# Attention block: output products of each head group in one slot, both key halves together

## What is computed

```python
q, k, v = qkv of _gn(x)
attn = jnp.einsum('bqd,bkd->bqk', q * scale, k)
attn = attn + rel_h[:, :, :, :, None] + rel_w[:, :, :, None, :]   # from q and two tables
attn = jax.nn.softmax(attn, axis=-1)
out = jnp.einsum('bqk,bkd->bqd', attn, v)
x = x + (out @ proj_w + proj_b)
```

## Time and profile before

| | |
|---|---|
| median of 3 runs | 1974.27 us (1973.04 to 1978.66) |
| the profiled execution's own time | 1973.15 us |
| its span, first to last instruction | 1971.3 us |
| mean granted TensorE clock | 0.996 |
| TensorE busy | 1904.9 us (97%) |
| VectorE, ScalarE, GpSimd busy | 1436.1, 1364.7, 713.3 us |
| `ps_o` matmuls | 6144 records, 340 ns each on the mean |

### The profile page before, as it was taken

The page is one execution under the profiler, slowest core; times in us unless marked ns, Lnnn a source line. Parts: engine busy times, 40 slices in busy tenths (PEclk is TensorE's granted clock), DMA queues, the critical chain, the costliest instruction groups (busy, mean ns, idle before and its releaser), DMA issues.

```text
span 1971.3 us, 85928 instructions
## 1 busy us (share of the span) xinstructions
PE 1904.9 (97%) x34944; PEld 1558.5 (79%) x34944; DVE 1436.1 (73%) x3566; ACT 1364.7 (69%) x3201; POOL 713.3 (36%) x1796
## 2 busy tenths in 40 slices
PE   0799999999999999999999999999999999999998
PEld 0688888888888888888888888888888888888885
DVE  6477777777777777777777777777777777777774
ACT  0277777777777777777777777777777777777775
POOL 0333433334334334334334333343343343343331
PEclk9999999999999999999999999999999999999999
DMA  1434444444444444444344344444444444444430
GB/s 38 101 93 110 103 100 110 103 102 108 104 100 109 103 102 107 102 107 105 100 110 104 99 110 106 100 104 108 100 107 104 101 108 102 107 104 100 112 97 23
DMA packets 142177, 197.86 MB, mean 100 GB/s; under 512 B 26455, under 2 KB 109656, under 8 KB 141786
## 3 DMA queue, kind: packets, MB, share of 16 engines
q1 hardware_dynamic: 141786, 192.36, 39.3%
HBM read 97.74 MB, written 57.80 MB: 79 GB/s over the span
## 4 chain that ended last, share of the span: by engine, by line
PE 93%; issue 3%; DVE 2%; POOL 1%; ACT 0%; DMA 0%; POOLq 0%; SPq 0%; DVEq 0%; ACTq 0%
PE ps_m L402 24%; PE ps_max L511 17%; PE ps_o L543 17%; PE ps_sc L524 13%; PE ps_m L463 10%; PE ps_m L477 6%; PE ps_m L419 2%; PE ps_m L487 2%; PE ps_m L468 1%; PE ps_m L425 1%; DVE k_st L658 0%; POOL yo L837 0%; DVE v_st L651 0%; POOL xn L814 0%; POOL xn_lo L827 0%
## 5 line engine op out<-in xcount | busy, mean ns | idle before, releaser
L701 DVE TENSOR_REDUCE mx<-ps_max 98x2 f32<-98x392 f32 x1536 | 834.9, 558 | 237.3 <-PE ps_max L511 223.4
L574 ACT ACTIVATE probs<-ps_sc 98x392 f32<-98x392 f32 x1536 | 735.4, 496 | 216.8 <-PE ps_sc L524 171.8
L511 PE MATMUL ps_max<-k_st,q_st 124*98 124x196 f16 x3072 | 538.1, 257 | 0.6 <-DVE mx L701 0.3
L524 PE MATMUL ps_sc<-q_st,k_st 125*98 125x196 f16 x3072 | 511.7, 247 | 0.6 <-ACT probs L574 0.5
L511 PEld LDWEIGHTS ps_max<-k_st,q_st 124*98 124x98 f16 x3072 | 293.8, 125 | 200.1 <-issue 157.6
L543 PE MATMUL ps_o<-probs,v_st 98*32 98x196 f32 x6144 | 388.7, 340 | 2.0 <-issue 1.2
L524 PEld LDWEIGHTS ps_sc<-q_st,k_st 125*98 125x98 f16 x3072 | 320.9, 124 | 3.4 <-ACT probs L574 1.8
L752 DVE TENSOR_TENSOR rel_hl<-ps_m,rel_hi 128x504 f16<-128x504 f32 (+1 forms) x384 | 216.2, 563 | 85.5 <-ACT rel_hi L619 85.5
L785 POOL TENSOR_TENSOR msq<-mv 96x2 f32<-96x2 f32 x128 | 24.6, 192 | 630.5 <-DVE mv L727 630.5
L619 ACT ACTIVATE rel_hi<-ps_m,is_lo 128x504 f16<-128x504 f32 (+1 forms) x384 | 225.7, 588 | 31.6 <-PE ps_m L463 31.3
L463 PE MATMUL ps_m<-q_st,rel_st 64*32 64x36 f16 (+1 forms) x14336 | 238.0, 208 | 0.2 <-DVE gsm L767 0.2
(11 more groups left out here) (72 smaller groups left out, 3051.3 us busy)
## 6 DMA issues: line engine op xcount, KB each, us to landing
q_st<-q_dram SPq DMA_DIRECT2D x128, 294.0 KB, 3.9
k_st<-k_dram SPq DMA_DIRECT2D x256, 147.0 KB, 3.9
q_dram<-qk_hl SPq DMA_DIRECT2D x128, 147.0 KB, 2.6
k_dram<-qk_hl SPq DMA_DIRECT2D x128, 147.0 KB, 2.8
q_st<-rel_hl SPq DMA_DIRECT2D x256, 73.5 KB
q_st<-rel_hl SPq DMA_DIRECT2D x256, 64.3 KB
xa<-in_x SPq DMA_DIRECT2D x64, 147.0 KB
x<-yo SPq DMA_DIRECT2D x64, 147.0 KB
```

The lines of the kernel that those rows point to most:

```text
L511: last = nc.tensor.matmul(ps_max[head % 2][0:HT, h * TOK:h * TOK + TOK], q_st[u.n % QB][0:R_MAX, head, h, :], k_st[u.n % QB][0:R_MAX, head ...
L524: last = nc.tensor.matmul(ps_sc[head % 2][0:HT, kt * TOK:kt * TOK + TOK], k_st[u.n % QB][0:STACK, head, kt * HT:kt * HT + HT], q_st[u.n % ...
L574: nc.scalar.activation(probs[head][:, :, :], ps_sc[head % 2][0:HT, 0:2 * TOK].rearrange("p (k t) -> p k t", k=2), ACT.Exp, scale=1.0 / (QS ...
L701: nc.vector.reduce_max(mx[u.r % 2][:, head, :], ps_max[head % 2][0:HT, 0:2 * TOK].rearrange("p (q k) -> p q k", q=2), axis=AX.X).then_inc( ...
```

## The change

`PV_AT` becomes one slot per group, both halves together: group 0 at 52 (slot 4) as before, group 1 at 56 (slot 8), group 2 at 60 (slot 0). ScalarE's copy follows at 53, 57 and 61, where it was 53, 57 and 62. A list `PV` of groups per visit is written in a general form, but each entry holds one group, so that tiles, banks and products stay the same. The three waits (`s_v`, `s_p`, `s_o`) that stood ahead of each group's first half now stand ahead of the whole visit, `s_v` for group 0 alone.

```diff
--- before.py
+++ after.py
@@ -247,7 +247,8 @@
         LEAD, TAIL = 2, 6
         MAX_AT, EXP_AT = 30, 47
 
-        PV_AT = {(0, 0): 52, (0, 1): 52, (1, 0): 55, (1, 1): 56, (2, 0): 59, (2, 1): 61}
+        PV = ((0,), (1,), (2,))
+        PV_AT = (52, 56, 60)
         O_LATER = 1
 
         JOBS = [(-10, "xT", 1, (s_xT, 1, 1)),
@@ -469,7 +470,7 @@
                                         ident[0:HT, 0:HT]).then_inc(s_mT_ps, 1)
                 elif name == "ot":
 
-                    pe.wait_ge(s_o, u.n * GROUPS + GROUPS)
+                    pe.wait_ge(s_o, u.n * len(PV) + len(PV))
                     bank_free(pe, unit, name)
                     for h in range(2):
                         for g in range(GROUPS):
@@ -529,21 +530,20 @@
                     for name in ORDER:
                         job(name, unit, s, layer)
 
-                    for (g, kt), at in PV_AT.items():
-                        u = due(unit, s, at)
+                    for i, groups in enumerate(PV):
+                        u = due(unit, s, PV_AT[i])
                         if u:
-                            n = u.n * GROUPS + g
-                            if kt == 0:
+                            if i == 0:
                                 wait(pe, s_v, u.n + 1)
-                                wait(pe, s_p, u.n * HEADS + HG * g + HG)
-                                wait(pe, s_o, n)
-                            for j in range(HG):
-                                head = HG * g + j
-                                p = probs[head]
-                                last = nc.tensor.matmul(ps_o[32 * j:32 * j + 32, 0:TOK],
-                                                        v_st[u.n % VB][:, kt, head_of(head), :], p[:, kt, :],
-                                                        start=kt == 0, stop=kt == 1)
-                            if kt == 1:
+                            wait(pe, s_p, u.n * HEADS + HG * groups[-1] + HG)
+                            wait(pe, s_o, u.n * len(PV) + i)
+                            for n, g in enumerate(groups):
+                                for kt in range(2):
+                                    for j in range(HG):
+                                        head = HG * g + j
+                                        last = nc.tensor.matmul(ps_o[32 * j:32 * j + 32, n * TOK:n * TOK + TOK],
+                                                                v_st[u.n % VB][:, kt, head_of(head), :],
+                                                                probs[head][:, kt, :], start=kt == 0, stop=kt == 1)
                                 last.then_inc(s_o_ps, 1)
 
             run(pe, iteration)
@@ -556,13 +556,14 @@
             def iteration(unit, layer):
                 for s in range(HEADS):
 
-                    for g in range(GROUPS):
-                        u = due(unit, s, PV_AT[g, 1] + O_LATER)
+                    for i, groups in enumerate(PV):
+                        u = due(unit, s, PV_AT[i] + O_LATER)
                         if u:
-                            act.wait_ge(s_o_ps, u.n * GROUPS + g + 1)
+                            act.wait_ge(s_o_ps, u.n * GROUPS + groups[-1] + 1)
                             wait(act, s_ot_ps, u.n - 1)
-                            nc.scalar.copy(o_sb[u.r % 2][:, g, :].rearrange("p (k r b) -> p k r b", r=2, b=SIDE),
-                                           ps_o[:, 0:TOK].rearrange("p (k b r) -> p k r b", r=2, b=SIDE))\
+                            nc.scalar.copy(o_sb[u.r % 2][:, groups[0]:groups[-1] + 1, :]
+                                           .rearrange("p g (k r b) -> p (g k) r b", r=2, b=SIDE),
+                                           ps_o[:, 0:len(groups) * TOK].rearrange("p (k b r) -> p k r b", r=2, b=SIDE))\
                               .then_inc(s_o, 1)
                     head = head_at(EXP_AT, s)
                     u = due(unit, s, EXP_AT + head)
```

## The result

The changed kernel takes 1978.67 us (median of 20 runs, 1976.58 to 1982.26) against 1973.55 us for the kernel before (20 runs, 1972.07 to 1978.66). The ratio is 1.0024, with a 95% interval of 1.0017 to 1.0031: a small loss, clear of zero and inside what the forecast called no change. 1976 us was forecast. The profiled execution's span is 1977.7 us, where it was 1971.3.

What follows compares the result with a forecast made beforehand. TensorE's start-to-start steps were taken to bound the kernel. From the profiled 1973.15 us, 35.7 lost, 34.6 gained and 2.6 lost make +3.7, less about 1 at start and end: 1976 us, range 1968 to 1990.

Steps and rivals of the forecast that it cites:

- The price of a visit, 0.27 us: Each run of ps_o matmuls on TensorE costs 0.09 entering, 0.14 leaving and 0.04 in the slot behind it.
- Group 1 costs 0.29 us a unit: Slots 7 to 9: without slot 7's visit, job g waits for VectorE's second rel_hl; 0.29 us a unit lost.
- Group 1's own steps, 0.18: Slots 7 and 8: counting only TensorE's own steps, one visit fewer would save 0.18 us a unit.
- 0.04 for the slot behind it: The slot after a visit is 0.38 instead of 0.34 us long, its first weight load not being fetched ahead.
- rival A: Slot 8: job g isn't held, so both groups save, 0.45 us a unit, 1917 us; chance 0.10.
- The length of the wait: Ahead of g in slot 8: TensorE stands still some 0.4 us, listed wait for rel_hl growing from 5.1 to some 45 us.
- The other signs: Over 100 g waits, 384 ps_o visits of 16, max(11) to max(3) 2.6 us, rel1's end to slot 9's max 0.29 longer.
- Slot 3: Slot 3's ps_max matmul reuses a bank VectorE is still reducing; 0.02 us a unit lost, bounds 0 and 0.05.
- rival B: Slot 3's ps_max or ps_sc is later than taken, 0.10 to 0.15 us a unit lost, 1992 us; chance 0.17.
- Rival C: Slot 8, behind g: the visit's own s_p and s_o waits aren't hidden, up to 0.08 us each, 1986 us; chance 0.12.
- The sum: Whole kernel: 35.7 us lost at group 1, 34.6 gained at group 2, 2.6 lost at slot 3; net +3.7 us.
- The 1 us that start and end were to give back: Units at the program's start and end, where g isn't held, were to return about 1 us.

Runs made afterwards that it cites:

- group 2 alone: Kernel before with only group 2 put in one visit (slot 0): 1942.50 us, ratio 0.9846.
- the split: Kernel before with group 0 split over slots 3 and 4 (one visit more) and job mT moved from slot 6 to slot 7: 2011.26 us.
- its control: Kernel before with only job mT moved from slot 6 to slot 7: 1976.47 us, ratio 1.0013.
- taking the wait away in the same order of instructions: Changed kernel with job g's result in PSUM bank 0 instead of 2: 1928.14 us, ratio 0.9772 to the kernel before.
- covering it again in slot 7: Changed kernel with the whole of group 1 in slot 7 instead of slot 8, g still in bank 2: 1911.57 us, ratio 0.9685 to the kernel before.
- group 1 alone: Kernel before with only group 1 put in one visit (slot 8): 2009.89 us, ratio 1.0187.

## Why the prediction came out right, point by point

**The price of a visit, 0.27 us.** Right: 0.261 with slot 3's share in it (group 2 alone), 0.268 by the split with its control. The drain that the Trainium skill (TensorEngine Tiling (Array Packing), Key Properties) states for a change of tiling mode agrees in kind with these numbers: all of these runs had the same 34944 matmul records, only more or fewer changes. The runs give the price of a whole visit; how much of it is such a drain isn't separated. Read as a forecast, that rule alone would have been wrong for group 1.

**Group 1 costs 0.29 us a unit.** Right to the hundredth, with its parts: 0.38 from rel_hl's end to the visit and 1.18 to slot 9's max, both as worked out. The sample of one held g at the end of the start-up was a good model for some 120 others. g itself came nearer to rel_hl's end by 0.09 us (0.24 before, 0.15 held), but a held g is followed by its visit 0.23 later and not 0.18, so that the visit behind it gained only the 0.04 that the prediction used. The cause is shown and not only argued: taking the wait away in the same order of instructions turned +0.290 into -0.10, and covering it again in slot 7 into -0.23 (-0.493 less -0.261).

**Group 1's own steps, 0.18.** The mechanism right, the size off: 0.14. The term "0.04 for the slot behind it" doesn't exist behind job rel. It didn't enter the forecast time, since g's wait covers it, but it is 5 of the 11 us by which rival A's time was too low: 1928 us was measured without the wait where that rival said 1917. Most of the rest is the 0.04 of job y.

**The length of the wait.** "Some 0.4 us" of standing still is 0.35 ahead of g and 0.04 ahead of y; but "some 45 us" in the list of waits is 27.4, because the list counts from modelled ends (0.18 a time in the row of g above). The other signs came: 126 waits, 384 visits of 16, 2.63 us from max(11) to max(3), and from rel1's start to slot 9's max 1213.48-1210.09 = 3.39 where it was 1209.13-1206.04 = 3.09. TensorE's busy time fell by 18.4 us, and g's listed wait grew by 22.3.

**Slot 3.** Only the trace answers rival B. The weight load of max(3) now stands 1218.41-1218.38 = 0.03 us ahead of its matmul, where it stood 1214.33-1214.25 = 0.08 ahead in the kernel before:

```profile
1214.25 0.21 PEld L511 LDWEIGHTS ps_max<-k_st,q_st 124*98 124x98 f16 x2
```

The changed kernel:

```profile
1217.76 1.59 DVE L702 TENSOR_REDUCE mx<-ps_max 98x2 f32<-98x392 f32 x3 [0.57 <-PE ps_max L512]
...
1218.38 0.17 PEld L512 LDWEIGHTS ps_max<-k_st,q_st 124*98 124x98 f16 x2
```

The reduction of max(1) starts at 1217.76, so with 0.56 ends at 1218.32 or a hundredth later, and the load comes at 1218.38, as worked out. The matmul stands 1218.41-1218.07 = 0.34 behind the first transpose, where four steps of 0.08 make 0.33. Of the lead, 0.05 us was slack, and the place costs some 0.01 us (group 2 came to 0.261 and not 0.27; a step of 0.01 is as fine as these rows are). 0.02 was taken.

**Rival C.** Right to be set aside: with g held, g to visit is 1212.68-1212.45 = 0.23 us, the same as in the earlier trace rows without the visit's own waits. With g not held it is 0.18 both with these waits (1208.62-1208.44, g in bank 0) and without them (1208.66-1208.48). There are no more semaphore instructions either: the recorded traces hold 1919 of them on TensorE's queue in both kernels.

**The sum.** In the steady part +0.029 us a unit, where the forecast's terms come to 0.29-0.27+0.02 = 0.04; the difference is slot 3, 0.01 for 0.02. That makes 3.5 us. It isn't two errors that cancel: each of the two large terms, some 35 us, was measured by itself and is right to 0.01 us a unit. The 1 us that start and end were to give back came out as a loss, of about 3 us in the profiled execution (6.4 less 3.5) and 1.6 by the medians (5.1 less 3.5). That is the step that the sum had wrong, in sign; the last section shows where a part of it comes from.

## What to carry to other kernels

Ahead of moving a piece of work, list who needs the engine to be late: the work that stood there was also the cover for a reader on another engine, and the slack behind it can be read from the timeline. Take the distance from the releaser's end to the instruction behind the one that may be held, and compare it with a place where that one really was held: here 0.42 and 0.38 us, so 0.04 of slack. The distance to g itself, 0.24 and 0.15, would have said 0.09. Two edits that look like one (fewer visits) can have opposite signs and add up to nothing; take them apart ahead of judging the idea. Here the idea was worth 3.2% once its second half stood one slot earlier.

## What wasn't expected of the hardware

The changed kernel's 9th g comes 2 us later than the kernel before's, though in the start-up too the order has changed by nothing but the visits. 1.6 of the 2 us come up between the 6th and the 7th g: 122.74-106.44 = 16.30 us against 120.83-106.09 = 14.74. The stretches of TensorE's clock from the two traces (stretch, length, busy us of each engine and their instructions, then the granted share, DMA share and GB/s) show what happens there. The changed kernel:

```profile
100.00:106.00 6.00, 5.16 (x129) 3.98 (x126) 4.39 (x13) 4.80 (x12) 0.38 (x2) 1.00 0.20 46
106.00:112.00 6.00, 5.56 (x78) 4.87 (x78) 2.97 (x8) 2.45 (x6) 4.23 (x11) 0.73 0.55 138
112.00:125.00 13.00, 12.82 (x255) 10.63 (x253) 9.72 (x25) 9.18 (x23) 1.83 (x7) 0.99 0.30 72
```

The kernel before, same stretches:

```profile
100.00:106.00 6.00, 5.27 (x133) 3.78 (x130) 4.42 (x13) 4.49 (x10) 0.39 (x2) 1.00 0.24 53
106.00:112.00 6.00, 5.91 (x99) 4.56 (x100) 3.87 (x9) 3.73 (x10) 4.25 (x11) 1.00 0.61 141
112.00:125.00 13.00, 13.00 (x255) 10.80 (x254) 9.62 (x25) 9.33 (x22) 3.62 (x12) 1.00 0.35 91
```

From 106 to 112 us the changed kernel has a mean clock of 0.73, that is the lower level (1.2 GHz) for about half of these six microseconds, where the kernel before keeps the full one. (In the recorded trace it is at that level from 108.79 to 112.20 us.) What TensorE did ahead of it: it stood 1.20 us before g at 106.44, where it stood 0.74 before.

```profile
106.44 0.30 PE L426 MATMUL ps_m<-mv,gmat 96*96 96x4 f32 x2 [1.20 <-DVE rel_hl L753]
```

The kernel with group 1 alone, which has the same long wait (1.22 us), shows 0.63 in that stretch. The nine other kernels' traces have no wait of TensorE over 0.75 us between the return to the full clock and 112 us, and all show 1.00 from 106 to 112. Among them is the changed kernel with g in bank 0, which has the same order of instructions without the wait. Later waits of 0.35 us, once a unit, left the clock at its full level: 1.00 from 112.2 to 1969 us. So the long wait and the lower clock come together in all eleven traces; each is one execution, and why the clock fell more than 2 us behind the end of the wait isn't shown.
